# A message-passing layer whose TensorE loop is written for two steps a turn instead of eight, with two-slot one-hot rings and one bank for picked tiles

## The chip, the cores and the metric

One core of one Trainium2 chip runs the whole program. The metric is the device time of one execution in microseconds.

## The reference, cut to what matters

The reference is a graph network of four layers over N = 3125 nodes with D = 128 features and E = 100000 edges, sorted by destination. The layers are a GIN layer, an attention layer (GATv2), a hypergraph layer and a message-passing layer. The change lies in the last one only. With the first weight matrix split into the part for the source, the part for the destination and one row for the edge weight, its messages are

    m[e] = silu(A[src[e]] + B[dst[e]] + ew[e] * row)
    acc[n] = sum over edges e with dst[e] = n of  ew[e] * m[e]   (and the sum of ew[e])

A and B are node tables that are ready before this stage (a linear map of the node features each). The edge term has the precision of three bf16 parts of a float32.

## The kernel before, in words

The nodes lie in WIN = 25 windows of P = 125. The edges lie in 800 tiles of 125, four tiles make a quad of 500 edges, so there are QUADS = 200. A quad that holds edges of two windows is worked on twice, which makes TEAMS = 224 steps. The function `message_sums` (L1020) gives each engine a program of its own; semaphores order them.

**POOL** fetches A[src] row by row with indirect DMAs (`gather_quads`, L593): four a quad, but three for every second quad, which comes to 700. The fourth tile of those 100 quads is *picked* instead: TensorE multiplies a one-hot matrix of the tile's source nodes with the table held on chip (`pick`, L1192; 25 matmuls of 384 columns, in halves of 13 and 12), DVE adds the three parts (`evict`, L1254), ACT writes the rows to memory (`store_picked`, L152), and SP reads them back into the quad's place (L152, in `fetch`). The rows lie in a ring of RING = 20 quads. **SP** (`pass_quads`, L597 to L629) tells POOL that a place is free once the step 18 quads back is added (L605, semaphore `kept`), and tells DVE that a quad is `here`.

In step k the other engines do this:

- **TensorE**, in its slot k: `spread_rows(k + 1)` (L1182, 12 matmuls: the one-hot matrix of destinations times the three parts of B and the row of edge weights, into half of `zp`), then one half of a picked tile, then `sum_team(k - 1)` (L1200, 4 float32 matmuls, 8 in the profile: the weighted one-hot matrix times the messages, into one half of `sums`). The loop's body is 8 steps (`batch`, L1222 with picks, L1224 without, for the last 24 steps), the first batch is written out ahead of it, and `windows_of` (L481) reads four window numbers from memory into registers, twice a turn.
- **DVE**, in step k: `add_rows(k)` (L1286, zp + gathered rows), `point` (L1249, the source one-hot of the next half tile, into `at`), at every second step `evict` of the tile that was finished before, and `add_team(k - 2)` (L1280, adds the sums to the window's row).
- **ACT**, in step k: `apply(k)` (L1100, silu; it waits for `added(k)` and for the sum of step k - 2), `load_spread(k + 3)` (L1083 and L1084, two DMAs into the ring `hot_t`), `widen(k + 2)` (L1094, four activations that scale the one-hot matrix by the edge weights into `onehot`; it waits for the sum of step k - 2, whose slot it takes), `load_hot(k + 4)` (L1088, into the ring `hot`), and at every second step `store_picked`.

The rings `hot`, `hot_t` and `onehot` have AHEAD = 4 slots, `zp`, `z`, `values` and `sums` two halves, and `mixture`, where the picked tiles are made, two banks, one per tile in turn. So `pick` of tile t waits until tile t - 2 is evicted. `at` holds one picked tile's one-hot matrix in two halves that are overwritten half by half.

Of the kernel before, what the change touches and what calls it, by code (L numbers as in the profile page):

```python
# [16 lines left out]
D = 128  # L17
# [1002 lines left out]
def message_sums(nc, g, table, at, pa, pb):  # L1020
# [7 lines left out]
    with Scope(nc) as sc:  # L1028
# [3 lines left out]
        hot_t = sc.sb("hot_t", [P + 3, AHEAD, HALF * P], BF16)  # L1032
        onehot = sc.sb("onehot", [P, AHEAD, HALF, P])
# [15 lines left out]
        mixture = sc.ps("mixture", [P, 2, 512])  # L1049
# [9 lines left out]
        hot_in, hot_t_in, ew_in = ([sc.sem(f"{x}{q}") for q in range(AHEAD)] for x in ("hot_in", "hot_t_in", "ew_in"))  # L1059
# [17 lines left out]
        def _(act):  # L1077
# [12 lines left out]
            def widen(k, m, q):  # L1090
                act.wait_ge(hot_in[q], landed(m))
                act.wait_ge(summed, after(k, AHEAD))
                for j in range(HALF):
                    ins = act.activation(onehot[:, q, j, :], hot[:, q, j * P:(j + 1) * P], ACT.Identity, scale=g.ew[:, bass.ds(HALF * k + j, 1)])  # L1094
                ins.then_inc(made, 1)
# [28 lines left out]
            def batch(b, storing=True, laying=True, loading=True, late=None, last=False):  # L1124
                for i in range(2):
                    first = steps * b + AHEAD * i
                    if not (last and i == 1):
                        quads = four_quads(first + AHEAD - 1)
# [19 lines left out]
            for q in range(AHEAD):  # L1148
                load_hot(q, q)
            quads = four_quads(0)  # L1150
            for q in range(3):
                load_spread(q, q, quads[q])
            lay(0)
            load_next(1)
            for q in range(2):
                widen(q, 0, q)
# [14 lines left out]
        def _(pe):  # L1171
# [3 lines left out]
            def spread_rows(k, m, q, w):  # L1175
                p = q % 2
                pe.wait_ge(hot_t_in[q], landed(m))
                pe.wait_ge(ew_in[q], landed(m))
                pe.wait_ge(added, after(k, 2))
                for j in range(HALF):  # L1180
                    for part in range(3):
                        ins = pe.matmul(zp[:, p, j, :], hot_t[:, q, j * P:(j + 1) * P], own_parts[:, part, bass.ds(w, 1), :].rearrange("p w f -> p (w f)"),  # L1182
# [3 lines left out]
            def pick(t, p, r):  # L1186
                lo, hi = halves[r]
                pe.wait_ge(noded, 2 * t + r + 1)
                if r == 0:
                    pe.wait_ge(evicted, t + 1)  # L1190
                for w in range(lo, hi):
                    ins = pe.matmul(mixture[:, p, 0:3 * D], hot_n[:, w, :], row_parts[:, w, :, :].rearrange("p k f -> p (k f)"), start=w == 0, stop=w == WIN - 1)  # L1192
                ins.then_inc(mixed, 1)

            def sum_team(k, q):
# [3 lines left out]
                for j in range(HALF):  # L1199
                    ins = pe.matmul(sums[:, q % 2, 0:width], onehot[:, q, j, :], values[:, q % 2, j, :], start=j == 0, stop=j == HALF - 1)  # L1200
                ins.then_inc(summed, 1)

            def batch(b, first=False, picking=True, last=False):
                for i in range(2):
                    ws = windows_of(nc, pe, g, steps * b + AHEAD * i + 1)
                    for q in range(AHEAD):
                        k, e = steps * b + AHEAD * i + q, AHEAD * i + q
                        if not (last and e == steps - 1):
                            spread_rows(k + 1, 2 * b + i + (q + 1) // AHEAD, (q + 1) % AHEAD, ws[q])
                        if picking:  # L1210
                            pick(SET * (b + 1) + e // 2, e // 2 % 2, e % 2)
                        if not (first and e == 0):
                            sum_team(k - 1, (q - 1) % AHEAD)

            pe.wait_ge(rows_ready, 1)
            for t in range(SET):
                for r in range(2):
                    pick(t, t % 2, r)
# [8 lines left out]
            sum_team(TEAMS - 1, AHEAD - 1)  # L1227

        @block.vector
        def _(dve):  # L1230
# [20 lines left out]
            def evict(t, m, p):  # L1251
                dve.wait_ge(mixed, 2 * t + 4)
                dve.wait_ge(stored[p], before(m, 16 * len(PIECES)))
                dve.tensor_reduce(picked[:, p, :], mixture[:, p, 0:3 * D].rearrange("p (k f) -> p f k", k=3), AX_X, ALU.add).then_inc(evicted, 1)  # L1254
# [33 lines left out]
            def batch(b, first=False, pointing=True, more=True, evicting=True, late=None):  # L1288
                for i in range(2):
# [6 lines left out]
                    for q in range(AHEAD):  # L1296
                        k, e = k0 + q, AHEAD * i + q
                        add_rows(k, q % 2, quads[q], slots[q])
                        if pointing and e < steps - 1:
# [7 lines left out]
                        if late is not None and e == 0:  # L1307
                            evict(late, late // 2, late % 2)
# [1564 lines left out]
```

## Time and profile before

| | |
|---|---|
| time, 3 runs | 6644.63, 6647.9, 6659.55 us, median 6647.9 |
| profiled execution | span 6634.5 us, no other time of it is shown |
| PE, DVE, ACT, POOL busy | 61%, 62%, 22%, 59% of the span |
| stage of the change | 5339.8 us (first gather) to 6572.2 us (last `add_team`) |

The profile comes from one execution. Its span runs from the first to the last thing recorded; times in the trace are counted from the span's start. Engines are PE (TensorE's matmuls), PEld (its weight loads), DVE, ACT, POOL and SP; a "q" behind a name is that engine's own sequence of register, branch and DMA-issuing instructions. L12 is line 12 of the kernel. "Idle before" is the time in which the engine did nothing ahead of those instructions, with what ended it; "issue" is idle time for which the profile shows no cause, and the name of a releaser is inferred from semaphore events. PEclk is the granted TensorE clock as a share of full speed. The ends of matmuls are modelled.

### The profile page before, as it was taken

How to read it: one execution, taken by the hardware profiler on the slowest of the kernel's cores; microseconds unless marked ns; L12 is line 12 of the kernel's file. 1: busy time of each engine (PE TensorE's matmuls, PEld its weight loads, DVE VectorE, ACT ScalarE, POOL GpSimd, SP SyncE). 2: the span in 40 equal slices, each digit the busy share in tenths (PEclk: the TensorE clock that was granted, in tenths of full speed). 3: DMA queues.
4: the chain of work that ended last, by engine and by line, in shares of the span. 5: the costliest groups of instructions: out<-in, count | busy, mean ns of one | idle time of the engine just before them, and what ended most of it. 6: DMA issues, size and time to landing. Idle time of an engine off the chain costs nothing. (4 is left out here: it accounts for less than half of the span.)

```text
span 6634.5 us, 118515 instructions
## 1 busy us (share of the span) xinstructions
PE 4017.4 (61%) x28023; PEld 3403.5 (51%) x28024; DVE 4113.0 (62%) x8988; ACT 1474.3 (22%) x3625; POOL 3943.0 (59%) x3172
## 2 busy tenths in 40 slices
PE   7878864555555534555555445555555457888886
PEld 5754433554445434545554345544444346666665
DVE  8987336666666676666666666666666664555554
ACT  4764000111111111111111101111112113343334
POOL 0000005888888738888888288888883067667762
PEclk9999985676666666667766666666676779999997
DMA  6853532333333323333333233333332223333332
GB/s 169 220 162 105 147 94 57 90 90 86 88 85 86 84 55 84 87 82 89 91 86 87 52 78 90 88 86 86 85 87 55 52 72 97 98 100 99 99 98 73
DMA packets 656905, 617.30 MB, mean 93 GB/s; under 512 B 246683, under 2 KB 595607, under 8 KB 656785
## 3 DMA queue, kind: packets, MB, share of 16 engines
q0 software_dynamic: 252480, 234.81, 15.3%
q10 hardware_dynamic: 254649, 235.22, 12.2%
q1 hardware_dynamic: 149655, 145.83, 8.2%
q8 instruction: 56, 0.92, 0.1%
q14 instruction: 65, 0.52, 0.0%
HBM read 520.46 MB, written 91.68 MB: 92 GB/s over the span
## 5 line engine op out<-in xcount | busy, mean ns | idle before, releaser
L593 POOL DMA_INDIRECT rows<-row_table,now x2400 | 3062.0, 1276 | 1562.5 <-issue 1541.5
L818 PE MATMUL sums<-both,hot 125*125 125x137 f32 x5376 | 1143.5, 375 | 1234.7 <-DVE acc L917 706.5
L818 PEld LDWEIGHTS sums<-both,hot 125*125 125x125 f32 x5376 | 978.6, 261 | 1325.1 <-issue 827.2
L593 POOL DMA_INDIRECT rows<-node_table,now x700 | 848.0, 1211 | 620.5 <-issue 564.8
L896 DVE TENSOR_TENSOR z<-zp,rows 125x528 f32<-125x528 f32 x672 | 475.6, 708 | 1000.6 <-SPq L618 423.6
L808 PE MATMUL zp<-parts,hot_t 125*125 x8100 | 863.9, 279 | 236.6 <-DVE z L896 146.6
L808 PEld LDWEIGHTS zp<-parts,hot_t 125*125 125x125 bf16 x8100 | 841.2, 189 | 264.7 <-issue 263.0
L750 ACT CAST hot<-hot 125x500 f32<-125x500 bf16 x672 | 408.5, 608 | 2170.7 <-PE sums L818 1409.7
L1192 PE MATMUL mixture<-row_parts,at 125*125 125x384 bf16 x2500 | 530.1, 360 | 80.5 <-DVE at L1249 44.0
L909 DVE TENSOR_TENSOR both<-rows,xl 125x512 f32 (+1 forms) x672 | 461.3, 687 | 102.8 <-issue 61.5
L899 DVE SCALAR_TENSOR_TENSOR z<-z,own 125x512 f32<-125x512 f32 x672 | 460.8, 686 | 1.7
L902 DVE TENSOR_REDUCE both<-z 125x16 f32<-125x512 f32 x672 | 457.4, 681 | 4.3
L1192 PEld LDWEIGHTS mixture<-row_parts,at 125*125 125x125 bf16 x2500 | 355.6, 151 | 203.2 <-issue 112.5
L1249 DVE TENSOR_TENSOR at<-spread_srcs,nodes 125x1625 bf16<-125x1625 f32 x200 | 356.7, 1785 | 155.2 <-DMA counts<-pairs 136.7
L1286 DVE TENSOR_TENSOR pb<-zp,rows 125x512 f32<-125x512 f32 x224 | 154.5, 690 | 418.3 <-remote 337.5
L1182 PE MATMUL zp<-own_parts,hot_t 128*125 x2688 | 272.4, 231 | 170.0 <-issue 149.5
L1182 PEld LDWEIGHTS zp<-own_parts,hot_t 128*125 128x125 bf16 x2688 | 220.1, 141 | 211.6 <-issue 209.3
L1528 DVE TENSOR_SCALAR hot<-nodes,both 125x522 bf16<-125x522 f16 x896 | 315.2, 415 | 16.8 <-PE bank L1567 16.7
L1094 ACT ACTIVATE onehot<-hot,ew 125x125 f32<-125x125 bf16 x896 | 284.3, 387 | 87.5 <-issue 73.9
L1567 PE MATMUL bank<-hot,hot_dst 125*125 125x261 bf16 x1792 | 259.4, 289 | 69.2 <-DVE hot L1528 37.2
L1200 PE MATMUL sums<-pb,onehot 125*125 125x129 f32 x1792 | 265.9, 288 | 8.5 <-issue 6.0
L1495 POOL DMA_DIRECT2D spread_slots<-slot_table x56 | 30.0, 535 | 391.1 <-DVE hot_t L1521 336.5
(466 smaller groups left out, 4701.4 us busy)
## 6 DMA issues: line engine op xcount, KB each, us to landing
hot_t<-hots_t ACTq DMA_DIRECT2D x902, 122.1 KB
hot<-hots ACTq DMA_DIRECT2D x896, 122.1 KB
rows<-row_table,now POOLq DMA_INDIRECT x2400
counts<-pairs SPq DMA_DIRECT2D x55, 685.1 KB
spread_slots<-slot_table POOLq DMA_DIRECT2D x56, 488.3 KB
hots_t<-hot_t SPq DMA_DIRECT2D x112, 218.8 KB
hots<-hot_dst SPq DMA_DIRECT2D x112, 218.8 KB
pairs<-cells SPq DMA_DIRECT2D x25, 685.1 KB
```

Of the source, the lines that this page charges most:

```text
L593: pool.indirect_dma_start(rows[:, q, j, :], None, table, bass.IndirectOffsetOnAxis(ap=now[:, n, lane + j:lane + j + 1], axis=0)).then_inc( ...
L750: act.copy(hot32[:, q % 2, :], hot[:, q, :]).then_inc(made, 1)
L808: ins = pe.matmul(zp[:, p, j, 0:ROW], hot_t[:, q, j * P:(j + 1) * P], own[part], start=part == 0 and j % 2 == 0, stop=part == 2, skip_grou ...
L818: ins = pe.matmul(sums[:, p, 0:ACCW], hot32[:, p, j * P:(j + 1) * P], values[:, p, j, :], start=j == 0, stop=j == HALF - 1)
L896: dve.tensor_tensor(z[:, p, :, :], zp[:, p, :, 0:ROW], rows[:, bass.ds(at, 1), :, :].rearrange("p a j f -> p (a j) f"), ALU.add).then_inc( ...
L899: dve.scalar_tensor_tensor(out=z[:, p, :, 0:D], in0=z[:, p, :, 0:D], scalar=0.0, in1=rows_of(own_att, HALF), op0=ALU.max, op1=ALU.mult).th ...
L902: dve.tensor_reduce(bent[:, p, :, :], z[:, p, :, 0:D].rearrange("p j (h c) -> p j h c", h=HEADS), AX_X, ALU.add).then_inc(reduced, 1)
L909: dve.tensor_tensor(values[:, q % 2, :, 0:D].rearrange("p j (h c) -> p j h c", h=HEADS), rows[:, bass.ds(at, 1), :, 0:D].rearrange("p a j ...
L1182: ins = pe.matmul(zp[:, p, j, :], hot_t[:, q, j * P:(j + 1) * P], own_parts[:, part, bass.ds(w, 1), :].rearrange("p w f -> p (w f)"), star ...
L1192: ins = pe.matmul(mixture[:, p, 0:3 * D], hot_n[:, w, :], row_parts[:, w, :, :].rearrange("p k f -> p (k f)"), start=w == 0, stop=w == WIN ...
L1249: dve.tensor_tensor(hot_n[:, lo:hi, :], src, each(nodes[:, lo:hi], P), ALU.is_equal).then_inc(noded, 1)
L1528: dve.tensor_scalar(hot[:, p % AHEAD, j, :], nodes[:, :], g.src_lo[:, s], g.src_unit[:, s], ALU.is_equal, ALU.mult).then_inc(hot_made, 1)
```

## The change

TensorE's loop takes two steps and one picked tile a turn. For that, slot numbers must repeat every two steps: `hot_t` and `onehot` get two slots instead of four (`hot` keeps four), and `mixture` has one bank. ACT's order moves closer to the use: in step k it loads `hot_t` for k + 2 (was k + 3), widens k + 1 (was k + 2; it now waits for the sum of step k - 1) and loads `hot` for k + 3 (was k + 4). `pick` of tile t waits for the eviction of tile t - 1 (was t - 2), and DVE evicts ahead of `point` instead of behind it. TensorE reads two window numbers at a time instead of four. POOL's and SP's programs are the same, as is the arithmetic.

```diff
-        hot_t = sc.sb("hot_t", [P + 3, AHEAD, HALF * P], BF16)
-        onehot = sc.sb("onehot", [P, AHEAD, HALF, P])
+        hot_t = sc.sb("hot_t", [P + 3, 2, HALF * P], BF16)
+        onehot = sc.sb("onehot", [P, 2, HALF, P])
...
-        mixture = sc.ps("mixture", [P, 2, 512])
+        mixture = sc.ps("mixture", [P, 512])
...
             def load_spread(k, q, quad):
-                act.wait_ge(spread, after(k, AHEAD))
+                act.wait_ge(spread, after(k, 2))
...
             def widen(k, m, q):
                 act.wait_ge(hot_in[q], landed(m))
-                act.wait_ge(summed, after(k, AHEAD))
+                act.wait_ge(summed, after(k, 2))
...
                         apply(k, q % 2)
-                        if not (last and e >= steps - 3):
-                            load_spread(k + 3, (q + 3) % AHEAD, quads[q])
                         if not (last and e >= steps - 2):
-                            widen(k + 2, 2 * b + i + (q + 2) // AHEAD, (q + 2) % AHEAD)
-                        if not (last and e >= steps - AHEAD):
-                            load_hot(k + AHEAD, q)
+                            load_spread(k + 2, q % 2, quads[q])
+                        if not (last and e >= steps - 1):
+                            widen(k + 1, 2 * b + i + (q + 1) // AHEAD, (q + 1) % AHEAD)
+                        if not (last and e >= steps - AHEAD + 1):
+                            load_hot(k + AHEAD - 1, (q + AHEAD - 1) % AHEAD)
...
-            def pick(t, p, r):
+            def pick(t, r):
                 lo, hi = halves[r]
                 pe.wait_ge(noded, 2 * t + r + 1)
                 if r == 0:
-                    pe.wait_ge(evicted, t + 1)
+                    pe.wait_ge(evicted, t + 2)
...
-            def batch(b, first=False, picking=True, last=False):
-                for i in range(2):
-                    ws = windows_of(nc, pe, g, steps * b + AHEAD * i + 1)
-                    for q in range(AHEAD):
-                        k, e = steps * b + AHEAD * i + q, AHEAD * i + q
-                        if not (last and e == steps - 1):
-                            spread_rows(k + 1, 2 * b + i + (q + 1) // AHEAD, (q + 1) % AHEAD, ws[q])
-                        if picking:
-                            pick(SET * (b + 1) + e // 2, e // 2 % 2, e % 2)
-                        if not (first and e == 0):
-                            sum_team(k - 1, (q - 1) % AHEAD)
+            def pair(i, first=False, picking=True, last=False):
+                ws = windows_of(nc, pe, g, 2 * i + 1, 2)
+                for q in range(2):
+                    k = 2 * i + q
+                    if not (last and q == 1):
+                        spread_rows(k + 1, i + q, 1 - q, ws[q])
+                    if picking:
+                        pick(i + SET, q)
+                    if not (first and q == 0):
+                        sum_team(k - 1, 1 - q)
...
-            batch(0, first=True)
-            with pe.Fori(1, SETS - 1) as b:
-                batch(b)
-            with pe.Fori(SETS - 1, batches - 1) as b:
-                batch(b, picking=False)
-            batch(batches - 1, picking=False, last=True)
+            pair(0, first=True)
+            with pe.Fori(1, MORE - SET) as i:
+                pair(i)
+            with pe.Fori(MORE - SET, TEAMS // 2 - 1) as i:
+                pair(i, picking=False)
+            pair(TEAMS // 2 - 1, picking=False, last=True)
...
                         add_rows(k, q % 2, quads[q], slots[q])
+                        if evicting and e % 2 == 0:
+                            t = e // 2 - 1
+                            evict(SET * (b + 1) + t, 2 * (b + 1) + t // 2, t % 2)
...
                         if pointing and e < steps - 1:
                             point(SET * (b + 1) + (e + 1) // 2, (e + 1) // 2, (e + 1) % 2)
...
-                        if evicting and e % 2 == 0:
-                            t = e // 2 - 1
-                            evict(SET * (b + 1) + t, 2 * (b + 1) + t // 2, t % 2)
```

## Rows read from the trace of the kernel before

**Rows 1.** DVE's adds and sums (L1286, L1280) and the picks (L1192): count, durations, first and last start
```profile
L1286 DVE TENSOR_TENSOR pb<-zp,rows x224: 681/691/693, 5405.2 to 6569.1; 125x512 f32<-125x512 f32 x112
...
L1280 DVE TENSOR_TENSOR acc<-acc,sums x224: 276/280/292, 5417.0 to 6571.9; 125x129 f32 x112
...
L1192 PE MATMUL mixture<-row_parts,at x2500: 322/327/582, 5361.3 to 6464.4; 125*125 125x384 bf16 x193
```

**Rows 2.** POOL's gathers (L593) from 5200 us on: their times, and idle time ahead of them
```profile
L593 POOL DMA_INDIRECT rows<-node_table,now x700: 1205/1209/1684, 5339.8 to 6516.6; - x175
...
  issue: 564.8, 659
  SPq L605: 54.8, 38
```

**Rows 3.** Stretches: window and its length, then busy us and count per engine, PEclk, DMA, GB/s
```profile
5405.00:5500.00 95.00, 72.79 (x425) 55.01 (x426) 38.83 (x47) 27.47 (x68) 75.92 (x63) 0.86 0.35 89
...
6100.00:6300.00 200.00, 169.15 (x1214) 138.07 (x1213) 106.96 (x133) 78.04 (x196) 140.02 (x116) 0.92 0.39 100
...
6465.00:6572.00 107.00, 79.80 (x642) 69.19 (x642) 31.66 (x68) 58.13 (x157) 41.09 (x34) 0.84 0.36 101
```

**Rows 4.** The timeline of one step of TensorE, with start, us, engine, line
```profile
5812.68 0.85 PE L1182 MATMUL zp<-own_parts,hot_t 128*125 x12
...
5813.38 2.28 PE L1192 MATMUL mixture<-row_parts,at 125*125 125x384 bf16 x13
...
5815.49 1.05 PE L1200 MATMUL sums<-pb,onehot 125*125 125x129 f32 x8
```

**Rows 5.** The groups by line, 5500 to 6400 us, with the idle time before them
```profile
L1249 DVE TENSOR_TENSOR at<-spread_srcs,nodes 125x1625 bf16<-125x1625 f32 (+1 forms) x166 | 296.2, 1784 | 122.8 <-DMA counts<-pairs 109.2 <-issue 7.1 <-PE mixture L1192 4.2
...
L1094 ACT ACTIVATE onehot<-hot,ew 125x125 f32<-125x125 bf16 x664 | 210.9, 387 | 66.0 <-issue 61.9 <-PE sums L1200 1.7 <-PE zp L1182 1.2
L1182 PE MATMUL zp<-own_parts,hot_t 128*125 x1989 | 201.7, 228 | 123.4 <-issue 121.5
...
L1286 DVE TENSOR_TENSOR pb<-zp,rows 125x512 f32<-125x512 f32 x166 | 114.4, 689 | 304.8 <-remote 275.4 <-issue 17.3 <-PE zp L1182 12.1
L1100 ACT ACTIVATE pb<-pb 125x512 f32<-125x512 f32 x166 | 104.5, 629 | 418.3 <-DMA row_table<-xr 316.8 <-DVE pb L1286 56.9 <-PE sums L1200 25.1
...
L1254 DVE TENSOR_REDUCE pb<-mixture 125x128 f32<-125x384 f32 x83 | 45.5, 548 | 0.0
```

**Rows 6.** The timeline about a paused step: TensorE's own rows
```profile
5693.76 2.28 PE L1192 MATMUL mixture<-row_parts,at 125*125 125x384 bf16 x13
5695.87 1.05 PE L1200 MATMUL sums<-pb,onehot 125*125 125x129 f32 x8
```

**Rows 7.** The timeline of all engines a little later
```profile
5701.64 1.86 DVE L1249 TENSOR_TENSOR at<-spread_srcs,nodes 125x1625 bf16<-125x1625 f32 x1 [2.86 <-DMA counts<-pairs]
...
5703.20 0.63 ACT L1100 ACTIVATE pb<-pb 125x512 f32<-125x512 f32 x1 [6.06 <-DMA row_table<-xr]
...
5704.66 0.30 PE L1182 MATMUL zp<-own_parts,hot_t 128*125 x2 [0.49 <-issue]
```

**Rows 8.** The page's DMA queue that carries instructions: packets, MB, share of 16 engines
```profile
q8 instruction: 56, 0.92, 0.1%
```

**Rows 9.** TensorE's sequencer: reads of window numbers (L481) and the loop's branch (L1222)
```profile
L481 PEldq TENSOR_LOAD <-steps x57: 545/1003/1317, 5398.5 to 6561.4; - x57
...
L1222 PEldq COMPARE_BRANCH  x23: 76/213/220, 5514.9 to 6465.2; - x23
```

**Rows 10.** The timeline near the end, steps without picks: loads of hot_t, and their use
```profile
6522.38 0.50 ACTq L1083 DMA_DIRECT2D hot_t<-hots_t  x1
...
6524.51 0.27 ACTq L1083 DMA_DIRECT2D hot_t<-hots_t  x1
...
6526.29 1.03 PE L1182 MATMUL zp<-own_parts,hot_t 128*125 x12 [0.44 <-DMA hot_t<-hots_t]
...
6529.78 1.04 PE L1182 MATMUL zp<-own_parts,hot_t 128*125 x12 [1.51 <-DMA hot_t<-hots_t]
```

More of the change, by code:

```diff
@@ L1058, in message_sums @@
         staged = [sc.sem(f"staged{n}") for n in range(STAGES)]
-        hot_in, hot_t_in, ew_in = ([sc.sem(f"{x}{q}") for q in range(AHEAD)] for x in ("hot_in", "hot_t_in", "ew_in"))
+        hot_in = [sc.sem(f"hot_in{q}") for q in range(AHEAD)]
+        hot_t_in, ew_in = sc.sems("hot_t_in"), sc.sems("ew_in")
         block = sc.block()
@@ L1091, in widen @@
                 act.wait_ge(hot_in[q], landed(m))
-                act.wait_ge(summed, after(k, AHEAD))
+                act.wait_ge(summed, after(k, 2))
                 for j in range(HALF):
-                    ins = act.activation(onehot[:, q, j, :], hot[:, q, j * P:(j + 1) * P], ACT.Identity, scale=g.ew[:, bass.ds(HALF * k + j, 1)])
+                    ins = act.activation(onehot[:, q % 2, j, :], hot[:, q, j * P:(j + 1) * P], ACT.Identity, scale=g.ew[:, bass.ds(HALF * k + j, 1)])
                 ins.then_inc(made, 1)
@@ L1127, in batch @@
                     if not (last and i == 1):
-                        quads = four_quads(first + AHEAD - 1)
+                        quads = four_quads(first + 2)
                     for q in range(AHEAD):
@@ L1147, in _ @@
             load_srcs(0)
-            for q in range(AHEAD):
+            for q in range(AHEAD - 1):
                 load_hot(q, q)
             quads = four_quads(0)
-            for q in range(3):
+            for q in range(2):
                 load_spread(q, q, quads[q])
@@ L1154, in _ @@
             load_next(1)
-            for q in range(2):
-                widen(q, 0, q)
+            widen(0, 0, 0)
             lay(1)
@@ L1181, in spread_rows @@
                     for part in range(3):
-                        ins = pe.matmul(zp[:, p, j, :], hot_t[:, q, j * P:(j + 1) * P], own_parts[:, part, bass.ds(w, 1), :].rearrange("p w f -> p (w f)"),
+                        ins = pe.matmul(zp[:, p, j, :], hot_t[:, p, j * P:(j + 1) * P], own_parts[:, part, bass.ds(w, 1), :].rearrange("p w f -> p (w f)"),
                                         start=part == 0 and j == 0, stop=part == 2, skip_group_check=True)
                 ins.then_inc(spread, 1)
-            def pick(t, p, r):
+            def pick(t, r):
                 lo, hi = halves[r]
@@ L1189, in pick @@
                 if r == 0:
-                    pe.wait_ge(evicted, t + 1)
+                    pe.wait_ge(evicted, t + 2)
                 for w in range(lo, hi):
-                    ins = pe.matmul(mixture[:, p, 0:3 * D], hot_n[:, w, :], row_parts[:, w, :, :].rearrange("p k f -> p (k f)"), start=w == 0, stop=w == WIN - 1)
+                    ins = pe.matmul(mixture[:, 0:3 * D], hot_n[:, w, :], row_parts[:, w, :, :].rearrange("p k f -> p (k f)"), start=w == 0, stop=w == WIN - 1)
                 ins.then_inc(mixed, 1)
@@ L1253, in evict @@
                 dve.wait_ge(stored[p], before(m, 16 * len(PIECES)))
-                dve.tensor_reduce(picked[:, p, :], mixture[:, p, 0:3 * D].rearrange("p (k f) -> p f k", k=3), AX_X, ALU.add).then_inc(evicted, 1)
+                dve.tensor_reduce(picked[:, p, :], mixture[:, 0:3 * D].rearrange("p (k f) -> p f k", k=3), AX_X, ALU.add).then_inc(evicted, 1)
             dve.wait_ge(laid, 1)
@@ L1298, in batch @@
                         add_rows(k, q % 2, quads[q], slots[q])
+                        if evicting and e % 2 == 0:
+                            t = e // 2 - 1
+                            evict(SET * (b + 1) + t, 2 * (b + 1) + t // 2, t % 2)
+                        if late is not None and e == 0:
+                            evict(late, late // 2, late % 2)
                         if pointing and e < steps - 1:
@@ L1303, in batch @@
                             point(SET * (b + 2), 0, 0)
-                        if evicting and e % 2 == 0:
-                            t = e // 2 - 1
-                            evict(SET * (b + 1) + t, 2 * (b + 1) + t // 2, t % 2)
-                        if late is not None and e == 0:
-                            evict(late, late // 2, late % 2)
                         if not (first and e < 2):
```

15 lines of the change are left out of this document (7 added, 8 removed).

## Prediction, made before the changed kernel ran

> **What bounds the kernel now.** I read the sources of L1286, L1280 and L1192 first, to place the stage: the first add is at 5405.2 us, the last pick at 6464.4, the last window sum ends at 6571.9 + 0.3 = 6572.2 [rows 1]. What follows, 62.3 us to the span's end at 6634.5, does not change. The 200 steps with picks take (6464 - 5405) / 200 = 5.3 us each, the 24 without them 108 us.
>
> Next POOL's gathers: 700 of 1.209 us, each with 0.30 us ahead of it, so one every 1.513 us (63 in 95 us in the first stretch) [rows 2, 3]. Unhindered they would be done at 5339.8 + 700 x 1.513 = 6399. The last one starts at 6516.6 and ends at 6518. So POOL loses 119 us: it waits for places in the ring, which come free late because the steps are late (SyncE's L605 is named for 54.8 us, the rest stands as issue), and from its last gather to the stage's end another 54 us pass while 18 full quads are worked off. The gathers are therefore a floor, not the bound. A quad has 3.5 gathers, 5.3 us, but there are 224 steps for 200 quads: over the steps the floor is 1059 / 224 = 4.73 us a step, and POOL began 65 us ahead.
>
> Then a step of TensorE. One that flows takes 0.7 + 2.1 + 0.9 us from start to start, 3.6 us for the mean of both halves [rows 4], and DVE's work is 0.69 + 1.78 + 0.55 / 2 + 0.28 = 3.0 us, ACT's 0.63 + 4 x 0.39 + the issues of its DMAs, some 3.2 us [rows 1, 5]. None of them needs 5.3. TensorE's missing time is **issue**: 121.5 us ahead of L1182 from 5500 to 6400, in pauses such as the 0.49 us ahead of two matmuls, again and again, with two or three matmuls between [rows 5, 7]. In these bursts the others learn late what TensorE has done. The picks that end at 5696.0 release DVE's `point` at 5701.64, and the sum that ends at 5696.9 releases ACT at 5703.20 [rows 6, 7], 5.6 and 6.3 us later; DVE's waits of 304.8 and 122.8 us and ACT's of 418.3 us are mostly this, whatever releaser is named [rows 5].
>
> What stops TensorE's sequencer? The rows give two hints. The first stretch, where the first batch is straight-line code and the loop's first turn is new, is the slowest: 425 matmuls in 95 us, 4.5 a us, against 1214 in 200 us, 6.1 a us, once the turns repeat; POOL's pace and the DMA share do not differ [rows 3]. And the last stretch, with 20 matmuls a step instead of 32.5, has 6.0 a us with waits for loads instead of pauses [rows 3, 10]. A turn is 8 x 32.5 = 260 matmuls with as many weight loads, 520 instructions and some 70 for registers and waits; the tail's is 320 and some. So the supply of instructions to a long body fits, and the change cuts the body to a quarter, about 150. Against it: the queue that brings instructions from memory has 56 packets in the whole program [rows 8], so what is slow would have to be a level on the engine's side. By the Trainium skill (Runtime: NRT & Kernel Launch, Instruction fetch mechanics) TensorE's buffer holds 2048 instructions. By that rule the old turn of 590 fits already, a shorter one gains nothing, and the time would be that of the second rival or worse; the packet count agrees with it, the slow first stretch does not speak against it.
>
> **The change, part by part.** *Body of two steps.* If the pauses go, 5.3 us a step fall to what the next limit allows. It costs twice the reads of window numbers (1.0 us) and four times the branches (0.21 us) [rows 9]: 4 x 1.21 - (2 x 1.0 + 0.21) = 2.6 us for eight steps, 0.33 a step, 74 us in all if nothing hid them. The wait for `hot_t` behind them (next part) hides them: they come ahead of it in the sequencer. With that cover gone the step would be 3.6 + 0.33 = 3.9 us, still under the gathers. I put 0.
>
> *Rings of two and the shorter look-ahead.* This is the new limit. `widen(k + 1)` now waits for sum k - 1, the last thing in TensorE's slot k, and everything behind it on ACT waits too: `load_hot(k + 3)`, then `apply(k + 1)`, then the load of `hot_t` for k + 3, which TensorE needs at the start of slot k + 2. From the end of a sum to that issue lie four activations of 0.39 us, 1.5 us (with a store, at odd steps, up to 0.9 more; between 1.0, if the sequencer runs ahead of the engine, and 2.4) [rows 5]. From issue to use the trace of before shows only the tail, where TensorE waited for it: 6522.38 to 6526.29 and 6524.51 to 6529.78, 3.9 and 5.3 us [rows 10]. So x = 1.5 + 3.9 = 5.4 up to 1.5 + 5.3 = 6.8 us after the end of one slot the spread of the slot after next can begin, and that slot ends 3.6 us later: two steps in x + 3.6, one in 4.5 to 5.2 us. I take 4.7, near the shorter wait, since the tail with its 2.7 us steps issues these loads closer together than a step of 4.7 does. `hot` is loaded earlier than its use by two steps and stays out of this; SP's and POOL's instructions are the same.
>
> *One bank for the picked tiles.* Between the end of a tile and the first pick of the next lie a sum and a spread, 0.9 + 0.85 = 1.8 to 1.9 us [rows 4]. DVE needs 0.69 for the add in front and 0.55 for the eviction [rows 5], 1.24 us, hence its new place ahead of `point`: hidden, with 0.6 us to spare, so 0; uncovered it would be at most 0.55 x 100 = 55 us. The eviction also waits for the store of two tiles before, issued one pair of steps earlier, over 7 us. The Trainium skill (Perfetto Trace Analysis, Matmuls) has independent matmul groups rotate through PSUM banks so that the eviction of one overlaps the next. By that rule the 55 us would be lost; by the rows of the flowing step nothing is.
>
> *Sum.* Stage end = 5405 + 200 x 4.7 + 24 x (5.4 + 1.9) / 2 (88 us) + 8 for the last step's way through ACT and DVE = 6441. That is above the gathers' floor (6399 and about 8), 131 us under 6572. From the span of 6634.5 that gives 6503; the runs' median is 13.4 us above the span, so 6517, and with a little for bursts that stay in the first turn **6520**. Its own range: 4.5 us a step lets the gathers decide, 6407 to 6411, 6485; 5.2 us gives 6541 to 6555, about 6625.
>
> **The rivals.**
> 1. *Late signals meet a shorter look-ahead (slower).* The pauses and late signals come from something else than the body's length, say what the gathers or other traffic share with TensorE, and stay. Before, `widen` and the loads had two more steps in hand; now the lateness L of a sum adds to x: the step is (5.4 + L + 3.6) / 2. It decides from L = 1.6 us on, where this passes 5.3. With L = 3, half of what [rows 6, 7] show, as if every second step were late (the 304.8 us ahead of L1286 are 1.8 us a step in the mean [rows 5]), it is 6.0 us: 5405 + 1200 + 96 = 6701, 129 us more, 6777; with L = 1.9 it is 5.45, 6680; with 6 in every step 7.5, some 7080. For it: a gap of 5.6 us ahead of DVE's `point` cannot come from DVE, and gathers run through both slow stretches, but only through half of the last one, which has no pauses [rows 2, 3]. Against it: the first stretch is slow at the same gather pace.
> 2. *No change.* The pauses stay but signals are late only where they were already waited for, and the chain of 4.5 to 5.2 us hides beneath 5.3: 6648, within 13 us. That is also the case that the change does nothing to what it aims at.
> 3. *Half gained.* The pauses go and ACT's chain is the slower one of its bounds, or the single bank costs its 55 us: 6560 to 6635. It is a gain still.
>
> **How the numbers follow.** Forecast with its own range 0.45; half gained 0.13; no change 0.10; late signals 0.32, a third of it under 6740. A measurement of this kernel can tell about 0.2%, 13 us, from no change. Faster by more: 0.45 + 0.13 = 0.58, same 0.10, slower 0.32. For 8 in 10 the range runs from 6480, just under the gathers' floor, to 6740; above it lie the rest of the late signals, 0.2.
>
> **What would show it.** Right: idle "issue" ahead of L1182 falls to a few us per 100 steps, matmuls in the stage go from 6.1 to about 7 a us, steps with picks are 4.6 to 4.8 us apart, TensorE's waits name hot_t or ew_rows, DVE's `point` starts within a us of the picks' end, POOL's last gather starts near 6400 to 6440, and the first stretch is no slower than the later ones. Wrong: pauses of the same shape with bodies of 150 instructions; L1286 and L1100 still idle "remote" or behind DMAs named at random; waits of TensorE for `evicted` (then the bank), or for `made` (then `widen`); POOL's last gather after 6516. If the pauses go and the time does not, the chain through ACT is dearer than 5.2 us a step and the working of the look-ahead failed.

## The result, and the profile after

The changed kernel takes 6879.8 us (median of 4 runs, 6866.3 to 6884.6) against 6648.0: a ratio of 1.034, with a 95% interval of 1.033 to 1.036. The forecast was 6520 us, faster, with a range up to 6740; the change made the kernel slower by 232 us.

The sources of the stage's lines, as in [rows 1, 2] (line numbers moved by a few):

```profile
L1278 DVE TENSOR_TENSOR acc<-acc,sums x224: 277/280/292, 5444.7 to 6820.0; 125x129 f32 x112
...
L1284 DVE TENSOR_TENSOR pb<-zp,rows x224: 683/692/693, 5431.5 to 6815.0; 125x512 f32<-125x512 f32 x112
...
L1191 PE MATMUL mixture<-row_parts,at x2500: 323/326/578, 5377.8 to 6671.1; 125*125 125x384 bf16 x193
...
L593 POOL DMA_INDIRECT rows<-node_table,now x700: 1205/1209/1680, 5356.3 to 6723.1; - x175
```

One number given ahead of this has to be set right: 192 steps carry picks and 32 do not, and not 200 and 24. Four of the 100 tiles are picked before the first step, the other 96 take two steps each, and in both traces 192 spreads start before the last pick. So a step with picks takes (6671.1 - 5431.5) / 192 = 6.5 us, against (6464.4 - 5405.2) / 192 = 5.5 before, and POOL's last gather starts at 6723 instead of 6517. The span is 248 us longer, and the stage ends 248 us later, at 6820.3 instead of 6572.2. Of these, 26 us are there at the first add, 180 come in the steps with picks and 41 in the 32 steps after them (149 us instead of 108). The groups by line from 5500 to 6300 us, to be read beside [rows 5]:

```profile
L1191 PE MATMUL mixture<-row_parts,at 125*125 125x384 bf16 x1550 | 348.8, 388 | 1.9 <-issue 1.6 <-DVE pb L1252 0.2
...
L1095 ACT ACTIVATE onehot<-hot,ew 125x125 f32<-125x125 bf16 x496 | 157.0, 387 | 447.7 <-PE sums L1199 292.6 <-issue 116.4 <-DMA row_table<-xr 38.8
L1181 PE MATMUL zp<-own_parts,hot_t 128*125 x1488 | 140.5, 256 | 226.3 <-DMA hot_t<-ew_rows 129.7 <-DMA hot_t<-hots_t 86.9 <-issue 9.7
```

TensorE's "issue" ahead of the spreads, 121.5 us in the 900 of [rows 5], is 9.7 us in 800 here. Read alone that looks like the forecast come true. But in its place TensorE waits 217 us for the two loads into `hot_t` (L1181), and ACT's widening waits 448 us, mostly for sums. A third thing stands in the means: a pick takes 388 ns, in the same stretch of the kernel before 356.

The granted clock over the same stretch is 0.84, against 0.93 before. Both stretches, the kernel before first:

```profile
5500.00:6300.00 800.00, 663.26 (x4781) 541.51 (x4780) 418.57 (x517) 310.62 (x774) 563.34 (x467) 0.93 0.39 99
...
5500.00:6300.00 800.00, 573.77 (x4024) 494.74 (x4025) 355.41 (x433) 254.37 (x650) 474.05 (x394) 0.84 0.32 83
```

### The profile page after: what moved, and what is told of

The parts are those of the page before. It is cut to its first block and busy times, and to the rows that moved or that the text cites. A ratio compares the mean times of both kernels' runs of the same rounds, so it can differ in the third digit from the quotient of the medians.

```text
span 6882.8 us, 119016 instructions
## 1 busy us (share of the span) xinstructions
PE 4036.9 (59%) x28023; PEld 3471.2 (50%) x28024; DVE 4125.0 (60%) x8988; ACT 1464.7 (21%) x3625; POOL 3954.8 (57%) x3172
## 5 line engine op out<-in xcount | busy, mean ns | idle before, releaser
L593 POOL DMA_INDIRECT rows<-row_table,now x2400 | 3073.4, 1281 | 1564.6 <-issue 1542.7
L593 POOL DMA_INDIRECT rows<-node_table,now x700 | 847.9, 1211 | 808.1 <-issue 649.1
L1191 PE MATMUL mixture<-row_parts,at 125*125 125x384 bf16 x2500 | 557.3, 385 | 63.2 <-DVE pb L1252 31.2
L909 DVE TENSOR_TENSOR both<-rows,xl 125x512 f32 (+1 forms) x672 | 461.0, 686 | 105.7 <-issue 61.1
L1181 PE MATMUL zp<-own_parts,hot_t 128*125 x2688 | 262.6, 261 | 404.1 <-DMA hot_t<-ew_rows 253.8
L1191 PEld LDWEIGHTS mixture<-row_parts,at 125*125 125x125 bf16 x2500 | 394.5, 165 | 162.7 <-issue 40.7
L1181 PEld LDWEIGHTS zp<-own_parts,hot_t 128*125 128x125 bf16 x2688 | 237.9, 167 | 430.7 <-issue 430.2
L1199 PEld LDWEIGHTS sums<-pb,onehot 125*125 125x125 f32 x1792 | 260.7, 212 | 8.4 <-ACT onehot L1095 0.9
```

What stands on the lines that cost most here:

```text
L593: pool.indirect_dma_start(rows[:, q, j, :], None, table, bass.IndirectOffsetOnAxis(ap=now[:, n, lane + j:lane + j + 1], axis=0)).then_inc( ...
L909: dve.tensor_tensor(values[:, q % 2, :, 0:D].rearrange("p j (h c) -> p j h c", h=HEADS), rows[:, bass.ds(at, 1), :, 0:D].rearrange("p a j ...
L1181: ins = pe.matmul(zp[:, p, j, :], hot_t[:, p, j * P:(j + 1) * P], own_parts[:, part, bass.ds(w, 1), :].rearrange("p w f -> p (w f)"), star ...
L1191: ins = pe.matmul(mixture[:, 0:3 * D], hot_n[:, w, :], row_parts[:, w, :, :].rearrange("p k f -> p (k f)"), start=w == 0, stop=w == WIN - 1)
L1199: ins = pe.matmul(sums[:, q, 0:width], onehot[:, q, j, :], values[:, q, j, :], start=j == 0, stop=j == HALF - 1)
```

## The experiments

Sixteen runs followed, of ten kernels, each beside the kernel before on its own chip, and the chips turned out to be of two kinds: **the kernel before takes 6480 to 6487 us on four chips and 6644 to 6648 us on two occasions, the first measurement and that of e7 and e8.** So ratios are compared, and times only within a kind. I call the second kind *pausing*, for what TensorE does there, and the first *even*. Two reservations: the number of the first measurement's chip is not on record, so the two occasions may be one chip or two, and each chip was met on one occasion only, so that chip and occasion are not told apart.

| kernel | chip | us | ratio to before, 95% |
|---|---|---|---|
| changed (the result) | pausing | 6879.8 | 1.0344 (1.0332 to 1.0357) |
| c1, before again | even | 6482.7 | 0.9995 (0.9985 to 1.0006) |
| c2, changed again | even | 6840.9 | 1.0544 (1.0526 to 1.0563) |
| e1, e9, e13: body of four steps, else as before | even | 6481.7, 6484.7, 6488.1 | 1.0001, 0.9999, 0.9999 (within 0.9989 to 1.0011) |
| e2, changed, body of eight steps | even | 6836.1 | 1.0542 (1.0519 to 1.0565) |
| e3, e10, e14: changed, hot_t three ahead | even | 6480.0, 6488.6, 6490.4 | 1.0005, 1.0002, 1.0007 (within 0.9992 to 1.0017) |
| e4, before with one bank | even | 6481.6 | 1.0004 (0.9994 to 1.0013) |
| e5, before, hot_t two ahead | even | 6480.7 | 1.0000 (0.9991 to 1.0010) |
| e6, changed, store before widen | even | 6689.6 | 1.0333 (1.0309 to 1.0357) |
| e7, changed, load before apply | pausing | 6871.3 | 1.0343 (1.0325 to 1.0360) |
| e12, the same | even | 6849.4 | 1.0547 (1.0526 to 1.0567) |
| e8, changed, both moves | pausing | 6795.2 | 1.0223 (1.0206 to 1.0240) |
| e11, the same | even | 6673.9 | 1.0306 (1.0274 to 1.0339) |

### e1: the short body alone

```diff
-                for i in range(2):
-                    ws = windows_of(nc, pe, g, steps * b + AHEAD * i + 1)
-                    for q in range(AHEAD):
+            def four(i, first=False, picking=True, last=False):
+                ws = windows_of(nc, pe, g, AHEAD * i + 1)
+                for q in range(AHEAD):
...
+            with pe.Fori(1, (MORE - SET) // 2) as i:
+                four(i)
...
```

> The kernel before with TensorE's body cut from eight steps to four (about 295 instructions); rings of four, two banks, orders of ACT and DVE as before. Theory A (the pauses come from the length of TensorE's loop body; the slowdown of the change comes from the shorter look-ahead): pauses gone or at least halved, steps bound by the gathers, 6480 to 6560 us. Theory B (the pauses come from something the engines share with the gathers and do not depend on the body): 6648 us within 13, idle 'issue' ahead of the spreads still near 120 us from 5500 to 6400.

It took 6481.7 us, which is what theory A asks for, but the kernel before took 6479.5 beside it. The body's length does nothing to the time there: the gap had gone before anything was changed.

### c1: the kernel before, on a chip that does not pause

> The kernel before, unchanged, for its profile beside the others. If the first four experiments stand for the kernel in its undisturbed form: near 6480 us, no idle 'issue' of TensorE in the stage, signals of its sums and picks seen within 0.5 us, the stage bound by the gathers. If the pauses belong to the kernel: 6648 us and the rows of the first profile.

The groups by line from 5500 to 6300, then the stretches and the gathers' source of this kernel:

```profile
L1192 PE MATMUL mixture<-row_parts,at 125*125 125x384 bf16 x2112 | 394.6, 340 | 33.6 <-DVE at L1249 33.2
...
L1182 PE MATMUL zp<-own_parts,hot_t 128*125 x2124 | 168.0, 229 | 77.1 <-DVE pb L1286 72.9 <-DMA hot_t<-ew_rows 2.4 <-DMA hot_t<-hots_t 1.7
L1286 DVE TENSOR_TENSOR pb<-zp,rows 125x512 f32<-125x512 f32 x176 | 121.4, 690 | 313.3 <-SPq L618 293.9 <-issue 15.6 <-PE zp L1182 3.6
```

```profile
5405.00:5500.00 95.00, 91.91 (x795) 82.69 (x794) 72.53 (x86) 48.53 (x122) 75.79 (x64) 0.98 0.47 126
...
5500.00:6300.00 800.00, 688.92 (x5660) 609.05 (x5659) 477.88 (x605) 364.49 (x920) 638.68 (x530) 0.96 0.44 115
```

```profile
L593 POOL DMA_INDIRECT rows<-node_table,now x700: 1205/1209/1784, 5352.1 to 6411.9; - x175
```

There is no "issue" named ahead of the spreads and no "remote" ahead of the adds. DVE waits for SyncE's L618 (294 us), the word that a quad is here, so the rows on their way are the bound: 5352.1 + 700 x 1.513 = 6411, and the last gather starts at 6411.9. This is the floor that the prediction worked out, and the kernel before sits on it already. The first stretch, whose 425 matmuls in 95 us were my hint that new code is supplied slowly [rows 3], has 795 here, with the same code. The queue that brings instructions has 56 packets in this profile too, as in [rows 8]: the pauses did not go with more instructions fetched from memory.

### c2: the changed kernel, on a chip that does not pause

> The changed kernel, unchanged. If its slowdown is the chain through ACT and not late signals: 6820 to 6880 us also where the kernel before takes 6480, so a ratio of 1.05 to 1.06. If it is the late signals of the first profiles: under 6600 us where there are none.

6840.9 us, 1.054. The slowdown does not need late signals; it is larger without the pauses, since the kernel before gains 165 us from their absence and the changed one 39. Here is one pair of its steps in the timeline, TensorE, ACT and DVE:

```profile
6002.11 1.05 PE L1199 MATMUL sums<-pb,onehot 125*125 125x129 f32 x8
...
6003.00 0.86 PE L1181 MATMUL zp<-own_parts,hot_t 128*125 x12
6003.35 0.69 ACT L1095 ACTIVATE onehot<-hot,ew 125x125 f32<-125x125 bf16 x2 [6.01 <-PE sums L1199]
...
6003.69 2.28 PE L1191 MATMUL mixture<-row_parts,at 125*125 125x384 bf16 x13
...
6003.95 0.67 ACT L1095 ACTIVATE onehot<-hot,ew 125x125 f32<-125x125 bf16 x2
6004.37 0.86 ACTq L152 DMA_DIRECT2D more_rows<-pb  x2
...
6005.40 0.63 ACT L1101 ACTIVATE pb<-pb 125x512 f32<-125x512 f32 x1 [0.78 <-DVE pb L1284]
6005.49 0.29 ACTq L1084 DMA_DIRECT2D hot_t<-hots_t  x1
6005.81 1.05 PE L1199 MATMUL sums<-pb,onehot 125*125 125x129 f32 x8
6005.94 0.27 ACTq L1085 DMA_DIRECT2D hot_t<-ew_rows  x1
...
6010.00 1.03 PE L1181 MATMUL zp<-own_parts,hot_t 128*125 x12 [3.14 <-DMA hot_t<-ew_rows]
6010.87 3.80 PE L1191 MATMUL mixture<-row_parts,at 125*125 125x384 bf16 x12
...
6014.47 1.08 PE L1199 MATMUL sums<-pb,onehot 125*125 125x129 f32 x8
...
6015.39 0.86 PE L1181 MATMUL zp<-own_parts,hot_t 128*125 x12
```

Read it as the prediction's chain. The sum ends at 6003.16, the widening starts 0.19 us later and lasts 1.27; the store's issue stands until 6005.23, the loads go out at 6005.49 and 6005.94, and 4.06 us after the second one the spread starts. From the sum's end to the spread that is **x = 6.84 us**, where I had 5.4 to 6.8. Over the 62 waited spreads between 5500 and 6300 us, taken the same way, the mean is 7.40: 0.19 to the widening, 2.96 to the first load, 0.57 between the two, 3.67 to the spread. They are the spreads of every second step, the ones behind a store; the steps between wait for none.

What I did not have is the slot behind the wait. It takes 6010.00 to 6015.55, 5.55 us, where the one before took 3.86: its 12 picks last 3.80 us, 0.32 each, against 2.1 to 2.3 for 12 or 13 when it flows. That is the lower of the clock's two levels, 1.2 GHz, after an idle time of 3.1 us. The granted clock is 1.00 in the slot before and 0.53 over these picks:

```profile
6003.00:6006.80 3.80, 3.80 (x35) 3.35 (x33) 3.19 (x4) 1.90 (x5) 3.19 (x3) 1.00 0.37 86
...
6010.90:6014.40 3.50, 3.50 (x15) 2.53 (x13) 0.69 (x1) 0.00 (x0) 2.14 (x3) 0.53 0.29 82
```

The means show it for the whole stretch:

```profile
L1191 PE MATMUL mixture<-row_parts,at 125*125 125x384 bf16 x1563 | 343.9, 381 | 0.0
...
L1181 PE MATMUL zp<-own_parts,hot_t 128*125 x1499 | 139.9, 254 | 228.8 <-DMA hot_t<-ew_rows 183.0 <-DMA hot_t<-hots_t 45.6
```

```profile
5500.00:6300.00 800.00, 567.32 (x4062) 491.23 (x4059) 358.25 (x439) 258.76 (x662) 486.01 (x403) 0.85 0.33 85
```

The granted clock is 0.85 against 0.96 in c1. So a pair takes x plus a slow slot: 6.84 + 5.55 = 12.39 us, and from 6003.00 to 6015.39 it is 12.39. In the mean of the 62 it is 7.40 + 5.38 (against 3.87 for a slot without a wait), 6.4 us a step.

The 2.96 us to the first load are not the same each time. They are 2.1 us at every second of the waited spreads, as in the pair shown, and 3.3 and 4.3 at the others in turn. There ACT's own sequence reads four steps' quad numbers from memory (L635) between the store and the load, and once in eight steps the loop's turn and one more small DMA stand there too:

```profile
L635 ACTq TENSOR_LOAD <-steps x32: 1082/1116/1263, 5502.1 to 6295.4; - x32
```

A read takes 1.1 us, and the prediction has no term for it: it counts such reads for TensorE alone.

### e2: the changed kernel with the long body

```diff
-            def pair(i, first=False, picking=True, last=False):
-                ws = windows_of(nc, pe, g, 2 * i + 1, 2)
-                for q in range(2):
...
+            def batch(b, first=False, picking=True, last=False):
+                for i in range(4):
+                    ws = windows_of(nc, pe, g, steps * b + 2 * i + 1, 2)
+                    for q in range(2):
...
```

> The changed kernel with TensorE's body written out for eight steps again; rings of two, one bank, ACT's and DVE's new orders stay. Theory A: the pauses come back and add to the waits for hot_t and ew_rows: 6950 to 7150 us. Theory B (the body's length does nothing, the look-ahead everything): 6880 us within 20, with the same idle rows as the changed kernel.

6836.1 us and 1.0542, against 1.0544 for the changed kernel (c2): the length of the body is worth nothing on such a chip, in either kernel (e1, e2). The slot without a wait takes 3.87 us with both bodies. Theory B's number is 6880, for a pausing chip; what is met is its claim, that the time is that of the changed kernel, on an even one. No kernel with this long body and rings of two ran on a pausing chip.

### e3: the load moved ahead of the wait for the sum

```diff
-                        quads = four_quads(first + 2)
+                        quads = four_quads(first + 3)
...
-                        if not (last and e >= steps - 2):
-                            load_spread(k + 2, q % 2, quads[q])
+                        if not (last and e >= steps - 3):
+                            load_spread(k + 3, (q + 1) % 2, quads[q])
...
+            load_spread(2, 0, quads[2])
```

> The changed kernel with one thing moved: ACT loads hot_t and ew_rows for step k + 3 in step k, ahead of its wait for the sum, still into two slots. Theory A with the look-ahead as the cause of the slowdown: the 387 us that TensorE waits for these loads go, the gathers bound the stage, 6490 to 6570 us. Rival (the rings of two and the one bank throttle the loop whatever the order on ACT, and late signals remain): over 6700 us, with TensorE waiting for made or evicted instead.

6480.0 us, 1.0005. With two slots in the rings, one bank and a body of two steps, the whole 358 us are gone. In step k the slot for k + 3 is free as soon as spread k + 1 is done, which opens slot k, so ACT loses nothing by loading it before it stops for the sum. The changed kernel loads for that same spread one step later, behind the wait. What is left of the new waits (lines, 5500 to 6300 us) lies under the gathers:

```profile
L1192 PE MATMUL mixture<-row_parts,at 125*125 125x384 bf16 x2150 | 410.4, 345 | 83.5 <-DVE pb L1253 82.6
...
L1182 PE MATMUL zp<-own_parts,hot_t 128*125 x2183 | 163.3, 226 | 19.3 <-DVE pb L1285 15.3 <-DMA hot_t<-ew_rows 2.3 <-DMA hot_t<-hots_t 1.0
```

### e4: one bank and the eviction's new place alone

```diff
-        mixture = sc.ps("mixture", [P, 2, 512])
+        mixture = sc.ps("mixture", [P, 512])
...
-                    pe.wait_ge(evicted, t + 1)
+                    pe.wait_ge(evicted, t + 2)
```

The rest of the edit puts `evict` ahead of `point` on DVE.

> The kernel before with one bank for the picked tiles and the eviction ahead of point, nothing else. If the bank costs nothing: 6648 us within 13. If late signals bite at the bank (the eviction is on TensorE's path now, and it learns late that the tile is made): one wait of 1 to 4 us per tile, 6700 to 6900 us.

```profile
L1192 PE MATMUL mixture<-row_parts,at 125*125 125x384 bf16 x2137 | 405.7, 343 | 94.0 <-DVE pb L1254 93.5
```

6481.6 us: no cost. But the row corrects my working: TensorE does wait for the eviction, 93.5 us in 800, a good microsecond per tile. The steps are 4.5 us apart there because of the gathers (178 adds in 800 us), not 3.6, and DVE's add comes when the rows are here, so the eviction behind it comes late too. These waits lie in time that the gathers leave over; what one bank costs a loop that TensorE itself bounds was not measured.

### e5: the kernel before, with the load two steps ahead

```diff
-                            load_spread(k + 3, (q + 3) % AHEAD, quads[q])
+                            load_spread(k + 2, (q + 2) % AHEAD, quads[q])
...
```

(The reads of quad numbers and the loads ahead of the loop are moved by one step with it.)

> The kernel before with one thing changed: hot_t and ew_rows are loaded for step k + 2 in step k instead of k + 3; rings of four, widen two steps ahead, two banks, eight steps. Theory 'the combination' (the load is late because it stands behind the widening, which waits for the sum just being made): the load is issued right after apply(k), TensorE waits a little, 6480 to 6520 us. Theory 'two steps are too few in themselves': 6600 us or more.

6480.7 us, 1.000. TensorE waits for the loads (row below, 88 us in 800 against 4 in c1), hidden under the gathers. So "two ahead" is not the fault in itself: it is two ahead *and* behind a widening that stops for the newest sum.

```profile
L1182 PE MATMUL zp<-own_parts,hot_t 128*125 x2148 | 183.4, 233 | 100.3 <-DMA hot_t<-ew_rows 72.5 <-DMA hot_t<-hots_t 15.5 <-DVE pb L1286 8.1
```

### e6, e7 and e8, e11 and e12: shorter ways from the sum to the load

e6 moves the store, e7 and e12 the load, e8 and e11 both:

```diff
+                        if storing and e % 2:
+                            store_picked(SET * (b + 1) + e // 2 - 1, (e // 2 + 1) % 2)
                         if not (last and e >= steps - 1):
                             widen(k + 1, 2 * b + i + (q + 1) // AHEAD, (q + 1) % AHEAD)
...
-                        if storing and e % 2:
-                            store_picked(SET * (b + 1) + e // 2 - 1, (e // 2 + 1) % 2)
```

```diff
-                        apply(k, q % 2)
                         if not (last and e >= steps - 2):
                             load_spread(k + 2, q % 2, quads[q])
+                        apply(k, q % 2)
```

> The changed kernel with the store of a picked tile (0.85 us of ACT's queue at every second step) ahead of the widening instead of behind it. If every microsecond between the end of a sum and the next load counts in full on every second step: 0.85 to 1.0 us less at each of 100 pairs of steps, 85 to 100 us under the changed kernel. If the wait for the load is set elsewhere: no change.

e6 took 6689.6 us, 151 less than c2 beside it, and more than the 85 to 100 expected. The store's 0.85 us is on the chain in full (the mean x falls from 7.40 to 6.48, the way to the first load from 2.96 to 1.91), and the clock gives back the rest: the wait of the second step falls from 3.7 to 2.5 us, its slot from 5.4 to 4.6 in the mean, and the picks in this row are at 357 ns, the clock at 0.93.

```profile
L1191 PE MATMUL mixture<-row_parts,at 125*125 125x384 bf16 x1800 | 361.2, 357 | 0.9 <-DVE pb L1252 0.8
```

> The changed kernel with the load of hot_t and ew_rows for step k + 2 ahead of apply(k) instead of behind it. In the changed kernel's second profile the load goes out 3.1 us after the widening starts in the mean, of which the widening is 1.3 and the store 0.6; the rest is apply waiting for DVE's add (which stands behind the eviction and point) and the reload of ACT's function table. If that rest is on the chain: 1.1 us less at each of 112 pairs of steps, some 120 us under the changed kernel, 6680 to 6760 us. If only the store and the widening count: no change, 6840 us.

> The load ahead of apply alone, once more, for the other kind of chip. Without pauses: 6680 to 6760 us if apply's wait is on the chain, 6840 us if only the store and the widening count. On a pausing chip: 6871 us within 15 again.

e7 took 6871.3 us on a pausing chip and e12 6849.4 on an even one, ratios 1.034 and 1.055 as for the changed kernel: no gain. Although the load now stands ahead of `apply`, it goes out 2.9 us after the widening's start in the mean (3.0 before), and `apply` merely 1.2 us later still. So `apply`'s wait for DVE was not on the chain, nor was the reload of ACT's function table; the queue ahead of the load was, with the store and the reads of L635.

> Both small moves on ACT: the load ahead of apply, the store ahead of the widening. Only the widening is left between the end of a sum and the load, x is 0.2 + 1.1 + 0.5 + 3.7 = 5.5 us, the pair of steps 5.5 + 3.7 = 9.2 us plus what the low clock adds after the wait (1.7 us in the changed kernel, less after a shorter wait). Chain theory: steps of 4.7 to 5.2 us, 6490 to 6600 us. Rival (one bank or rings of two hold the loop at 5.3 us a step or more): 6660 us or more.

> The two small moves on ACT once more, for the other kind of chip. Without pauses, chain theory: 6490 to 6600 us, under the 6690 of the store's move alone. On a pausing chip: 6795 us within 15 again.

e8 and e11 took 6795.2 and 6673.9 us, far above the 6490 to 6600 of the chain theory and inside the range of the rival, which blames the one bank or the rings of two. It is not the rival all the same: e3 has the same bank and rings and runs at 6480. Nor is a gain over e6 shown: the ratios are 1.0306 (1.0274 to 1.0339) and 1.0333 (1.0309 to 1.0357), and the four runs of e11 lie between 6643 and 6711. In e11's profile, which is of its fastest run, x is 6.36 in the mean, where I had counted 5.5. Of the difference 0.67 us lies between the widening's start and the load, 1.77 instead of 1.1: 0.95 at every second waited spread, and 2.2 and 3.1 in turn at the others, where the reads of L635 stand between, as in c2.

### e9, e10, e13, e14: in search of a pausing chip

> The kernel of the first experiment (body of four steps, all else as before) once more, beside the kernel before on this chip. On a chip where the kernel before takes 6645 us and its TensorE pauses: theory A (the body's length makes the pauses) 6480 to 6560 us, theory B (the chip makes them, whatever the body) 6645 us within 13. On a chip where the kernel before takes 6480 us: 6480 again, and nothing is told apart.

> The changed kernel with hot_t loaded three steps ahead, once more. On a pausing chip: theory A 6480 to 6560 us, since the body is of two steps; theory B 6645 us or some more, as the single bank and the later widening have less in hand against late signals, 6650 to 6750 us. On a chip without pauses: 6480 us.

> The body of four steps, all else as before, in the hope of a pausing chip. There: theory A (the body's length makes the pauses) 6480 to 6560 us, theory B (the chip makes them whatever the body) 6645 us within 13. On a chip without pauses 6480 us, which tells nothing apart.

> The changed kernel with hot_t loaded three steps ahead, in the hope of a pausing chip. There: theory A 6480 to 6560 us; theory B 6645 to 6750 us, with TensorE's idle issue back near 12 us per 100 us. On a chip without pauses 6480 us.

All four fell on even chips and took 6484.7 to 6490.4 us, like the kernel before beside them. They repeat e1's and e3's numbers and tell nothing on what the body's length does on a pausing chip. What e8 shows on the pausing chip, with a body of two steps, is this (timeline):

```profile
5998.93 1.05 PE L1199 MATMUL sums<-pb,onehot 125*125 125x129 f32 x8
...
6003.29 2.33 PE L1191 MATMUL mixture<-row_parts,at 125*125 125x384 bf16 x13 [0.86 <-issue]
```

```profile
6004.33 0.69 ACT L1095 ACTIVATE onehot<-hot,ew 125x125 f32<-125x125 bf16 x2 [6.03 <-DMA row_table<-xr]
```

Late signals are still there: the sum that ends at 5999.98 releases the widening at 6004.33, 4.35 us late, where it is 0.19 in c2; over the waited spreads of this stretch the mean is 1.24. The short pauses, though, are nearly gone. From 5500 to 6300 us the kernel before has 309 gaps of "issue" over 0.2 us ahead of TensorE's matmuls, 128 us with a median of 0.43. With a body of two steps on the pausing kind there are 4 (the changed kernel, 11 us), 5 (e7, 13 us) and 14 (e8, 25 us). That is what the forecast asked of a short body. Whether the body did it, or the waits for the loads that these three kernels have and the kernel before has not, no run tells: for that the long body with rings of two (e2), or the short one without these waits (e3), would have to run on a pausing chip.

## Why the prediction was wrong

The step that failed is the size of the chain by the short look-ahead: it was put at 4.7 us a step and measured 6.4. The prediction names this case itself, among its signs: "If the pauses go and the time does not, the chain through ACT is dearer than 5.2 us a step".

- **The gathers' floor: right.** 1.513 us a gather, a stage end of 6407 to 6411 and a time near 6485 were in the text. In c1 the last gather starts at 6411.9 and the stage ends at 6419.6, after a first gather 12 us later; c1, e1, e3, e4 and e5 lie at 6480 to 6483. On an even chip it is the kernel before that runs at it.
- **"What stops TensorE's sequencer ... the supply of instructions to a long body fits": not borne out as it stands, and open for the rest.** A long body alone makes no pauses: eight, four and two steps take the same time on even chips (e1, e2), and the straight-line first batch runs at 795 matmuls in 95 us. Both hints that I took from [rows 3] came from one execution on one pausing chip. That the queue of instructions had 56 packets [rows 8], with pauses and, in c1, without, spoke against my reading and weighed too little. The Trainium skill (Runtime: NRT & Kernel Launch, Instruction fetch mechanics) gives TensorE's buffer 2048 instructions. By that rule a body of about 590 fits, and e1 and e2 agree. On the pausing kind the forecast's own sign did come, short pauses nearly gone with a body of two steps, and its cause was not isolated. What makes a chip pause is open too. Had the forecast been met in time on such a chip, the reason given for it would still not have been shown.
- **The chain by the short look-ahead: the right mechanism, mis-sized, and it was the whole effect. This step failed.** "One in 4.5 to 5.2 us" came out at 6.4. x was 7.4 instead of 5.4 in the mean. The first load goes out 3.0 us after the widening's start where 1.5 was counted: 1.0 for the widening's issue, 1.05 for the store (by e6), which I named for odd steps and then left out of the value taken, and 0.85 in the mean for the reads of L635 and the loop's turn on ACT, which I did not have at all. Then 0.57 + 3.67 = 4.2 us follow instead of 3.9, and the signal takes 0.2. And the slot behind the wait costs 5.4 us instead of 3.6, because the wait takes the clock down. (7.4 + 5.4) / 2 = 6.4. I costed a wait as the wait alone.
- **The chain above the gathers' floor: right in order, wrong in size.** The text put its end at 6441, 34 us above the floor, and it came at 6820 (6777 in c2, against 6420 in c1). POOL then waits for it (SyncE's L605 is named for 105.7 us from 5500 to 6300 in the changed kernel, against 5.5 in c1). Experiment e3 shows that cause by removing it, on even chips. The sum also counted 200 steps with picks and 24 without; with 192 and 32 it comes out 9 us lower, which changes nothing here.
- **The reads of window numbers and branches on TensorE, 0: right as far as tested.** e1 doubles the turns, and e3 has four times the turns and twice the reads, both at no difference beyond 0.2%, though under the gathers; e2 takes the turns back in the slower kernel and gains nothing.
- **One bank, 0: right in the sum, wrong in the reason.** TensorE waits for the eviction (e4), but under the gathers. The Trainium skill (Perfetto Trace Analysis, Matmuls) has independent matmul groups rotate through banks; by that rule one bank would have cost 55 us in my working. e4 measured nothing, with the gathers as the bound.
- **Rival 1, slower: right in the place, wrong in the price's cause.** Its formula with a lateness L of 3 us gave 6777, and a shorter look-ahead on ACT was the place. But L is 0.19 us in c2, where the loss is larger, and 0.46 in the mean over the waited spreads of the result's own trace. What it put down to late signals was the store, the reads, the longer way to the load and the low clock.

## What to carry to other kernels

When a load is issued by an engine whose program stops for a late signal, count the look-ahead from that stop and not in steps, with everything that stands between in its queue: with the same two slots, the load ahead of the wait was free here and behind it cost 358 us. A wait that idles TensorE is to be charged with the slower work after it: 3.1 to 3.7 us of waiting cost 1.5 to 1.7 us more in the next slot here. And before a change is aimed at idle time named "issue", the kernel should be timed on a second chip: here the gap was 2.5% of the time, and the same kernel ran without it on four chips.

## What was not expected of the hardware

The kernel before takes 6480 to 6487 us on four chips and 6644 to 6648 us on two other occasions, each time by no more than some 0.2% around its median. On the slower kind the trace shows TensorE's idle "issue" in short pauses and its semaphores reaching ACT and DVE 4 to 6 us late. It is this stage that is slow there (4781 matmuls from 5500 to 6300 us against 5660 in c1): its first gather starts at 5339.8 us, 12 us before that of c1. The changed kernel loses only 39 us to it. It waits for its loads anyway, and its short pauses are nearly gone, for a reason that no run shows.
